# Retention layers and a mixture of experts on one core: z and h change layout by VectorE's block transposes and DMA instead of TensorE's transposes

## What is computed

```python
def block(h, p):
    r = _retention(h, wk)              # tril(q k^T)/row norm/denominator @ v
    m = r @ w1 + b1
    a, gate = jnp.split(m, 2, axis=-1)
    m = a * jax.nn.silu(gate) @ w2 + b2
    m = _groupnorm1(m, gg, gb)
    y = m + h
    f = jax.nn.gelu(y @ wf1 + bf1_, approximate=False) @ wf2 + bf2_
    return _layernorm(f + y, lg, lb), None      # f + y is called z below
out, _ = jax.lax.scan(block, x, params)         # 4 layers
x = _layernorm(x + out)
x = _layernorm(x + experts(x))
```

## Time and profile before

| | |
|---|---|
| median of 3 runs | 2429.43 us (2429.24 to 2431.05) |
| profiled execution | 2427.29 us |
| its span | 2425.6 us |
| TensorE matmul busy | 2398.8 us (99%) |
| VectorE, ScalarE, GpSimd busy | 1548.2, 1367.1, 1356.7 us |
| DMA | 106822 packets, 287.64 MB, mean 119 GB/s |

### The profile page before, as it was taken

How to read it: one execution, slowest core, us unless ns; L and a number is a source line. 1 busy time by engine, 2 the same in 40 slices (tenths; PEclk the granted TensorE clock), 3 DMA queues, 4 the chain that set the end, 5 groups by cost and what they waited for, 6 DMA issues and landing times. The chain is left out here.

```text
span 2425.6 us, 35215 instructions
## 1 busy us (share of the span) xinstructions
PE 2398.8 (99%) x11674; PEld 2007.9 (83%) x11674; DVE 1548.2 (64%) x2877; ACT 1367.1 (56%) x2403; POOL 1356.7 (56%) x1255
## 2 busy tenths in 40 slices
PE   9999999999999999999999999999999999999998
PEld 7888888888888888878888888888888888888886
DVE  4666666666666666778787856665646656564445
ACT  5666766667666666666655544444444444444443
POOL 2355655455544644567888955545545546554444
PEclk9999999999999999999999999999999999999999
DMA  7011121111100112127665564544445443444442
GB/s 252 27 52 43 36 79 35 35 35 46 58 26 17 36 44 70 35 89 233 238 208 191 181 224 145 185 149 160 149 161 186 159 153 145 154 151 169 152 161 74
DMA packets 106822, 287.64 MB, mean 119 GB/s; under 512 B 7360, under 2 KB 77248, under 8 KB 90304
## 3 DMA queue, kind: packets, MB, share of 16 engines
q1 hardware_dynamic: 105856, 285.16, 34.2%
q10 hardware_dynamic: 832, 0.82, 0.1%
HBM read 216.36 MB, written 69.60 MB: 118 GB/s over the span
## 5 line engine op out<-in xcount | busy, mean ns | idle before, releaser
L711 POOL TENSOR_TENSOR hid_lo<-full,hid_hi 128x512 fp32r<-128x512 f32 x384 | 504.8, 1329 | 514.9 <-ACT full L1015 462.7
L1520 DVE SCALAR_TENSOR_TENSOR full<-ps,bias_cols,sum 128x512 f32<-128x512 f32 x384 | 288.2, 750 | 218.2 <-PE ps L1799 198.6
L1797 PE MATMUL ps<-hid_hi,m_w 128*128 128x512 f32 x1024 | 401.8, 392 | 0.1
L1799 PE MATMUL ps<-hid_hi,m_w 128*128 128x512 f32 x1024 | 398.8, 389 | 0.0
L1798 PE MATMUL ps<-hid_lo,m_w 128*128 128x512 f32 x1024 | 398.5, 389 | 0.0
L1012 ACT ACTIVATE hid_hi<-ps,bias_cols 128x512 fp32r<-128x512 f32 x128 | 88.3, 690 | 496.6 <-PE ps L1799 496.6
L1797 PE MATMUL ps<-te_hi,m_w 128*128 128x512 f32 x896 | 351.1, 392 | 1.6 <-DVE sum L1507 0.9
L1799 PE MATMUL ps<-te_hi,m_w 128*128 128x512 f32 x896 | 348.9, 389 | 0.0
L1798 PE MATMUL ps<-te_lo,m_w 128*128 128x512 f32 x896 | 348.6, 389 | 0.0
L1799 PEld LDWEIGHTS ps<-hid_hi,m_w 128*128 128x128 f32 x1024 | 192.2, 188 | 40.5
L1797 PEld LDWEIGHTS ps<-hid_hi,m_w 128*128 128x128 f32 x1024 | 192.3, 188 | 39.5 <-issue 0.5
(11 more groups left out here) (212 smaller groups left out, 5586.0 us busy)
## 6 DMA issues: line engine op xcount, KB each, us to landing
m_w<-prepared SPq DMA_DIRECT2D x96, 1408.0 KB, 6.0
prepared<-m_w SPq DMA_DIRECT2D x32, 1408.0 KB, 5.8
h_store<-h_out SPq DMA_DIRECT2D x32, 512.0 KB, 3.2
we_raw<-in_W SPq DMA_DIRECT2D x64, 256.0 KB, 6.4
gate_bc<-gate_rows SPq DMA_DIRECT2D x64, 256.0 KB, 6.4
h_in<-h_store SPq DMA_DIRECT2D x24, 512.0 KB, 4.4
h_in<-in_x SPq DMA_DIRECT2D x8, 512.0 KB, 5.9
raw<-in_Wf SPq DMA_DIRECT2D x8, 512.0 KB, 8.4
```

Source lines behind the costliest of these rows:

```text
L711: nc.gpsimd.tensor_tensor(out=hid_lo[:, k, :], in0=full[:, k, :], in1=f32(hid_hi[:, k, :]), op=ALU.subtract).then_inc(hid_ready, 1)
L1520: nc.vector.scalar_tensor_tensor(out=full[:, k, :], in0=src, scalar=b1_col(e, 2 * fp + BLOCK_ROW[k]), in1=other[:, :], op0=ALU.add, op1=AL ...
L1797: nc.tensor.matmul(out, w[0], x[0], start=first, stop=False, skip_group_check=True)
L1799: return nc.tensor.matmul(out, w[1], x[0], start=False, stop=last, skip_group_check=True)
```

## The change

TensorE's transposes of h are gone, and those of z except in the last step. Instead:

- z: VectorE transposes each 128x512 half of `y` in blocks of 32x32 (`turn_z`) into the first half of `tmp`. SP stores the blocks at their places in `z_store` in HBM by four DMAs (`store_z`), one for each 32 partitions, in runs of 32 numbers (128 B), and loads z back in token layout (`load_z`). `gated` of the same slot waits until the store has read `tmp`.
- h: VectorE transposes `h_out` in the same way into the tile `z` (`turn_h`), SP stores it to `hT_store` (`store_hT`), and hT is later loaded from there to `hT_in`, which both slots share (`load_hT`). h itself is stored and loaded as before. `high_hT` and `low_hT` now read `hT_in` in all layers, and stand earlier: B's behind high_r(A) and low_r(A), the next step's A's behind high_y(A, 1) and low_p(B).
- The LayerNorm of slot B is finished one step later: its moments, rstd, normalise_z and layernorm_out are those of the step two back (`earlier`).
- ScalarE: keep_z is gone; normalise_z(A) and normalise_z(B, earlier) stand right behind high_t(B), ahead of the copies of B's scores; two of these copies stand ahead of high_y(A, 0).
- GpSimd: layernorm_out(B, earlier) moves behind rstd_group(A), ahead of mask_scores(B); f2's low half in seams stands between the two.
- The layer's constants come by a small DMA into `lc`, not by VectorE's copy.
- project_t(B) keeps its place ahead of group_moments(A) and scores(B).

The core of the diff, cut:

```diff
+            def store_hT(s, it):
+                sp.wait_ge(h_turned, it * SLOTS + s + 1)
+                for r in range(P // BLOCK):
+                    sp.dma_start(hT_blocks[it + PAIRS, s, r],
+                                 z[s][r * BLOCK:(r + 1) * BLOCK, :, :].rearrange("p k (q a) -> p k q a", a=BLOCK)
+                                 ).then_inc(hT_stored[s], DMA)
+
+            def store_z(s, it):
+                sp.wait_ge(z_ready[s], it * U + U)
+                for q in range(P // BLOCK):
+                    sp.dma_start(z_blocks[s, q], turned_z(s)[q * BLOCK:(q + 1) * BLOCK, :, :].rearrange("p c (n b) -> p c n b", b=BLOCK)
+                                 ).then_inc(z_moved[s], DMA)
+
+            def load_z(s, it, turned=True):
+
+                sp.wait_ge(z_moved[s], it * Z_MOVE + Z_MOVE + Z_STORE)
+                if turned:
+                    sp.wait_ge(hT_stored[s], it * H_STORE + H_STORE)
+                sp.wait_ge(h_new[s], it * U + U)
+                sp.dma_start(z[s][:, :, :], z_v[s]).then_inc(z_moved[s], DMA)
...
+                store_z(A_, it - 1)
...
+                if earlier and turn:
+                    store_hT(A_, it - 2)
+                load_z(A_, it - 1, turn)
+                load(A_, it + 1)
+                load_T(A_, it + 1)
+                if earlier:
+                    store_h(B_, it - 2)
...
+                store_z(B_, it - 1)
...
+                load_T(B_, it + 1)
+                if earlier and turn:
+                    store_hT(B_, it - 2)
+                load_z(B_, it - 1, turn)
+                load(B_, it + 1)
+                store_h(A_, it - 1)
...
# ScalarE
+                    high_hT(B_, now)
                     hidden(B_, before)
...
+                high_t(B_, now)
+                if before:
+                    normalise_z(A_, before)
...
+                if earlier:
+                    normalise_z(B_, earlier)
                 if seam:
                     next_high_weight("f2", now.layer, f2_psum[B_], before)
...
-                high_p(B_, now, (0,))
+                high_p(B_, now, (0, 1))
                 high_y(A_, now, 0)
...
+                if not last:
+                    high_hT(A_, step_behind(act, now))
                 hidden(A_, now)
...
# VectorE
+            def turn_z(s, at, c):
+
+                dve.wait_ge(z_ready[s], at.base + residuals(s, c))
+                nc.vector.transpose(turned_z(s)[:, c, :], y[s][:, c, :]).then_inc(z_ready[s], 1)
+
+            def turn_h(s, at):
+
+                dve.wait_ge(h_new[s], at.base + 2 * U)
+                nc.vector.transpose(z[s][:, :, :].rearrange("p k d -> p (k d)"),
+                                    h_out[s][:, :, :].rearrange("p k d -> p (k d)")).then_inc(h_turned, 1)
...
# TensorE
-                if not entry:
-                    transpose_h(A_, now)
...
                 for c in range(DC):
                     project_t(A_, now, c)
                 if before:
-                    transpose_z(A_, before)
                     out_projection(B_, before)
...
                 for c in range(DC):
                     project_t(B_, now, c)
                 group_moments(A_, now)
                 if before:
-                    transpose_z(B_, before)
+                    scores(B_, now, range(TB), before)
```

More of the change, by code:

```diff
@@ L754, in body @@
                 if seam:
-                    for name in ("f1", "f2"):
-                        split_weight(name, now.layer)
+                    split_weight("f1", now.layer)
                 rstd_group(A_, now)
+                if seam:
+                    split_weight("f2", now.layer)
+                if earlier:
+                    layernorm_out(pool, nc.gpsimd, B_, earlier)
                 if last:
@@ L1033, in keep_out, with body @@
                                      ACT.Copy).then_inc(spare_free, 1)
-            def body(now, before, seam, last=False, entry=False):
+            def body(now, before, earlier, seam, last=False, turn=True):
                 if seam:
@@ L1083, in body @@
                 high_u(A_, now, 1)
-                if before:
-                    high_hT(B_, now, entry)
-                else:
+                if not before:
                     for i in (1, 2):
@@ L1611, in body @@
                         residual(A_, before, c)
-                if seam:
-                    dve.wait_ge(z_ready[A_], before.base + U)
-                    hold(dve, held)
-                    next_constants(A_, now.layer)
-                if before:
-                    low_hT(A_, now, entry)
+                    for c in range(DC):
+                        turn_z(A_, before, c)
+                    if earlier and turn:
+                        turn_h(A_, earlier)
                     gated_products(B_, before)
-                low_t(A_, now, 0)
-                low_t(A_, now, 1)
+                for c in range(DC):
+                    low_t(A_, now, c)
                 if not before:
                     low_fold_vm()
-                    dve.wait_ge(consts_loaded, 2 * DMA)
-                    for s in range(SLOTS):
-                        next_constants(s, 0)
-                        dve.wait_ge(lc_ready[s], 1)
+                    dve.wait_ge(consts_loaded, DMA)
                 if before:
@@ L1641, in body @@
                         sum_moments(0, t)
-                if seam:
-                    dve.wait_ge(lc_ready[A_], now.layer + 1)
+                if earlier:
+                    for blocks in HALVES:
+                        layernorm_stats(B_, earlier, blocks)
+                    layernorm_var(B_, earlier)
                 if before:
@@ L1655, in body @@
                     residual(B_, before, 1)
-                if seam:
-                    dve.wait_ge(z_ready[B_], before.base + U)
-                    hold(dve, held)
-                    next_constants(B_, now.layer)
                 low_t(B_, now, 0)
@@ L1663, in body @@
                 groupnorm_out(A_, now)
+                if before:
+                    turn_z(B_, before, 1)
                 low_p(B_, now, range(TB))
-                if before:
-                    for blocks in HALVES:
-                        layernorm_stats(B_, before, blocks)
-                    layernorm_var(B_, before)
+                if not last:
+                    low_hT(A_, step_behind(dve, now))
+                if earlier and turn:
+                    turn_h(B_, earlier)
                 for half in range(2):
```

329 lines of the change are left out of this document (160 added, 169 removed).

## The result

The changed kernel takes 2507.89 us (median of 4 runs, 2504.82 to 2508.17), the kernel before 2429.51 beside it: 1.0318 times as long, 95% interval 1.0301 to 1.0336. Slower was forecast, by 8 us; it is 78. The profiled execution has a span of 2506.4 us.

A forecast was written before the change was run, and what follows sets the result against it. TensorE was taken as the bound, busy 2398.8 of 2425.6 us. Eight steady steps at +0.2 (+1 to 2), layer 0 +2, seams +3.6, last step and tail +0.5 gave about +8: 2437 us, range 2415 to 2470.

The forecast's parts named there:

- What TensorE saves: Removed transposes on TensorE: 0.88 us a group, 2.65 per steady step for three groups, nothing won for z of B.
- ScalarE's order at up_projection(A): Normalising and score copies ahead of y(A)'s copy on ScalarE delay up_projection(A): +1.4 us a step.
- Slot A's u: ScalarE's copies of B's hT make gate(A) later, so TensorE stalls for u: 0.5 us (0.2 to 0.9).
- Moments of B: VectorE's added block transposes make slot B's moments late for TensorE: 0.4 us, bounds 0 and 1.2.
- The block transposes: VectorE's three added transposes before B's moments, estimated from similar-width instructions: 0.7, 0.7 and 1.2 us.
- the low halves of f(A): GpSimd's f(A) subtractions, with layernorm_out(B) now ahead of B's masks: 0.4 us with the second y half (0 to 1.2).
- Layer 0, seams, last step: Layer 0's two later steps 64.8 us each, three seams +1.2 each, last step and tail +0.5.
- DMA: Stores and loads of turned z and h: 18 ns per 128 B packet taken, z(A) 10 us early, no cost.
- (c): Layout's DMA becomes the bound, z late at layernorm_stats(A), above 28 ns a packet; 2671 at 47 ns; chance 0.06.
- (d): VectorE's statistics of A wait for z's DMA, counted as slower; not otherwise spelled out or sized; chance 0.12.
- (a): Transposes go, but handovers and ScalarE's order take all of it back: 2437, own range 2428 to 2450; chance 0.56.

The follow-up runs named there:

- t1: Changed kernel with layernorm_out(B, earlier) cut to one 128x4 GpSimd instruction, so slot B's LayerNorm gain and bias are missing from the output: 2450.3 us.
- t2: t1 with both normalise_z moved into ScalarE's idle time ahead of high_t(B): 2430.8 us.
- z1: e2 with layernorm_out(B, earlier) behind layernorm_out(A) at the step's turn, and turn_h(B), its stores and load of z(B) one step later: 2579.7 us.
- e2: Changed kernel with both normalise_z moved into ScalarE's idle time ahead of high_t(B), GpSimd's order kept: 2498.9 us.
- z4: z3 with GpSimd's split_h(A) waiting for low_u(B) and ScalarE copying hT(B) ahead of r(A): 2434.1 us.
- f1: z4, last step only: sum_moments(0, 1) and inverse_root(1) moved behind low_p(B), GpSimd's layernorm_out held until VectorE's normalise_x1 are done: 2423.5 us.
- z3: z1 with hT(B)'s store and z(B)'s load ahead of hT(A)'s load on SyncE, plus unused semaphore increments: 2442.0 us.
- d1: Changed kernel with every store of turned z and h issued twice, the second to memory nobody reads: 2521.2 us.

## Why the prediction was wrong

Right in direction, wrong in size: 2507.9 lies 38 us above the range. By its steps:

- *What TensorE saves.* Right: 0.90, 0.89 and 0.91 for the three groups, 0.88 forecast. The fourth, z of B, was called worthless; it gave 0.63 and its wait took 0.59: right.
- *ScalarE's order at up_projection(A).* Right: +1.4 forecast, 1.53 in the step (idle 1.36), and 19.5 us over the kernel (t1 to t2). up_projection(A) starts 680.39 - 673.98 = 6.41 behind the moments, 6.3 forecast.
- *Slot A's u.* +0.5 forecast, 0.49 found. *Moments of B:* +0.4 forecast, 0.13 found; this was too dear.
- *The block transposes.* Taken at 0.7, 0.7 and 1.2 us; measured medians 0.700 and 1.216. None was blocked. In z1 three of them run under GpSimd's two instructions of 2.4 us (from 739.16 and from 741.71) at their usual time, while the subtraction that follows is blocked until the second ends:

```profile
739.58 1.29 DVE L1398 STREAM_TRANSPOSE tmp<-y 128x512 f32<-128x512 f32 x2
740.79 1.20 DVE L1403 STREAM_TRANSPOSE z<-h_out 128x1024 f32<-128x1024 f32 x1
...
743.46 1.21 DVE L1252 TENSOR_TENSOR tu_sp<-tmp,tu_sp 128x512 fp32r<-128x512 f32 x1 [0.83 <-ACT tu_sp L975]
```

  The Trainium skill (SBUF — State Buffer, "Who interferes with whom") says just this: a VectorE instruction with at most one SBUF input, outside its two-port modes, doesn't contend; one with two SBUF inputs does with a GpSimd instruction that reads SBUF; and the order of issue decides who blocks. The trace agrees for the transposes (0.65 and 1.20 us) and for the subtraction (1.21 in place of 0.69). The blocked TENSOR_SCALARs of e2 and z4, which read one tensor and scalars from SBUF, are not explained by the runs.
- *The step that failed: "the low halves of f(A)", with "0.4 for this and the second y half together (0 to 1.2)".* The prediction saw that GpSimd's layernorm_out(B) would now stand there, and priced it as work on GpSimd's own path. For f(A) it was too little (0.95 in t2), and for another reason, since t2 has no layernorm_out(B); in the changed kernel the late y(A) covers it. For the second half of y(A) it should have asked which of VectorE's instructions would run at the same time, and with how many SBUF inputs. It cost 2.96 us of wait and 1.64 at the lower clock, in the next step 2.97 and 2.94: 4.6 to 5.9 a step where at most 1.2 stood. It asked the question of the new transposes, where the answer was harmless, and not of the old instructions beside the moved one. The answer was to be had in the trace of before, at the start of a step, where layernorm_out(B) stood then; VectorE's low_u(B), 0.69 us elsewhere, and GpSimd:

```profile
726.50 1.82 DVE L1203 TENSOR_TENSOR tu_sp<-tmp,tu_sp 128x512 fp32r<-128x512 f32 x1 [0.83 <-ACT tu_sp L913]
...
725.37 2.41 POOL L406 TENSOR_TENSOR h_out<-z,lnv 128x1024 f32<-128x1024 f32 x1 [0.23 <-POOL z L399]
```

  Its end, 728.32, is 727.78 + 0.54. There it cost nothing: TensorE shows no wait for this u.
- *Layer 0, seams, last step.* Layer 0's later steps are 70.1 and 68.9 us where 64.8 stood, and the three seams 3.1 to 5.9 longer than before where 1.2 stood; t1 takes 3.8 to 4.8 us of each back, so most of it is the same block. Step 1 has no earlier B and so no layernorm_out(B): it is 0.9 longer. The last step is 12.4 longer where 0.5 stood for it and the tail; f1 shows the block and VectorE's order there. In t1, without the block at y(A), the last step is still 8.4 longer than before (74.31 against 65.86). That is most of the 13 us by which t1 itself lies above the forecast of 2437.
- *DMA.* Right that it costs nothing, with 18 ns a packet taken and 13.7 measured. (c) and (d) are out: VectorE never waits for z in the changed kernel. By 13.7 ns for 128 B against 47 for 1 KB, small packets are 2.3 times as dear per byte. The Trainium skill's rule of read-modify-write under 512 B (DMA: Bandwidth & Descriptors, Specifications) stood beside rival (d) and its 36 ns; the runs show no such doubling. But the fixed part, the order in which SyncE waits, was the sharp edge: z1 fell over it.
- *The range.* Its upper end also had a slip: the high bounds of u, moments and f(A) together are +2.0 a step above the forecast (0.4 + 0.8 + 0.8), not 1.5. That moves 2458 to some 2465, and 2507.9 stays outside.
- *The rivals.* All of them spoke of the parts that the change touches by its layout. None was "a moved instruction blocks a neighbour engine". Chance (a) had 0.56 and its own range ended at 2450; t1, the changed kernel without the block, takes 2450.3.

In sum: 78.4 us = 57.6 (GpSimd's block with its clock spell, t1) + 19.5 (ScalarE's order, t2) + 1.3, the rest, in which steady steps gain some 0.9 each, and the last step (7.2 longer), the start and layer 0 (some 3 together) give it back. These are differences between runs and not independent of order, and t1 takes the work away together with its place: z3, which does the same work at another place, is 11.2 us above t2, 6.4 of them waits of VectorE for z.

## What to carry to other kernels

When an edit moves an instruction to "idle time" of VectorE or GpSimd, list what the other of the two does in that stretch: each VectorE instruction with two SBUF inputs there, a two-column one too, can be delayed by a whole GpSimd instruction (2.21 us in place of 0.16). When a move changes which transfer waits for whom on one queue, read the waits in queue order; some 140 us hung here on the order of a few lines that moved no byte more. And add to a wait of TensorE what it costs behind itself: some 0.2 us of restart (1.36 idle cost 1.53, 0.40 cost 0.59), and here 1.64 and 2.94 us of lower clock behind waits of 2.79 and 2.83.

## What the runs showed of the hardware

- VectorE's block transpose of fp32: 0.700 us for 128x512 (0.667 to 0.714, 60 of them), 1.216 for 128x1024 (1.201 to 1.233, 24), the price of a plain instruction of that width.
- The block by GpSimd went to the end of GpSimd's running instruction at every width of VectorE's seen here: 2.21 us for 128x2 (0.16 alone), 2.87 for 128x512 (0.75 alone). A TENSOR_SCALAR of 128x2 with SBUF operands was blocked as well (2.32), a SCALAR_TENSOR_TENSOR between two of GpSimd's instructions got through in 0.22.
- Packets of 128 B to HBM took 13.7 ns on a DMA engine, 147 GB/s on sixteen (d1).
- TensorE's clock: behind idles of 2.79, 2.83 and 3.81 us inside busy work the matmuls ran at 1.2 GHz (0.42 us apart), and two spells behind nearly the same idle differed, 1.64 and 2.94 us of loss; behind 1.48 and 1.36 us they ran on at 2.4 (0.23 apart).
